# Mixture-of-experts routing: top two logits by max and max-index, routing weights behind the row numbers, slot table on POOL

## The reference, cut to what matters

```python
probs = softmax(x @ gate_w.T)                 # x: 2048 x 256, 8 experts
w, idx = top_k(probs, 2)
w = w / sum(w)
combine = zeros((2048, 8)).at[arange(2048)[:, None], idx].add(w)
for e in range(8):
    g, u = split(x @ gate_up[e].T, 2)         # 256 -> 2 x 1024
    out += combine[:, e:e+1] * (silu(g) * u @ down[e].T)
```

## Time and profile before

| | |
|---|---|
| median of 3 runs | 556.72 us (552.91 to 558.14) |
| span of the profiled execution | 555.4 us |
| PE busy | 495.3 us (89%), weight loads 363.6 us (65%) |
| DVE busy | 386.1 us (70%) |
| ACT busy | 340.2 us (61%) |
| POOL busy | 273.4 us (49%) |
| attention stage / routing / expert stage | about 233 / 33 / 289 us |

### The profile page before, as it was taken

How to read it: one execution, slowest core, us unless ns; L and a number is a source line. 1 busy time by engine, 2 the same in 40 slices (tenths; PEclk the granted TensorE clock), 3 DMA queues, 4 the chain that set the end, 5 groups by cost and what they waited for, 6 DMA issues and landing times.

```text
span 555.4 us, 12114 instructions
## 1 busy us (share of the span) xinstructions
PE 495.3 (89%) x3741; PEld 363.6 (65%) x3756; DVE 386.1 (70%) x805; ACT 340.2 (61%) x642; POOL 273.4 (49%) x347
## 2 busy tenths in 40 slices
PE   4695889998999888799798999999999999999990
PEld 3463546775666555526566888878888888777750
DVE  5437458888888765788577997887667677666551
ACT  1220588888788888374675777766656566645530
POOL 5006464574564564203227566656567555644244
PEclk9986799999999989899999999999999999999996
DMA  7567757768658632563666777967555465554224
GB/s 215 191 171 174 239 147 231 203 171 264 192 170 253 200 118 76 179 204 112 152 137 111 158 129 195 180 120 157 94 104 86 85 84 101 96 68 77 30 30 47
DMA packets 88090, 79.89 MB, mean 144 GB/s; under 512 B 49176, under 2 KB 73368, under 8 KB 87896
## 3 DMA queue, kind: packets, MB, share of 16 engines
q1 hardware_dynamic: 76512, 63.38, 41.8%
q0 software_dynamic: 11520, 15.74, 17.6%
HBM read 49.08 MB, written 22.41 MB: 129 GB/s over the span
## 4 chain that ended last, share of the span: by engine, by line
PE 67%; DVE 10%; ACT 7%; DMA 5%; issue 5%; SPq 3%; POOL 2%; another core or an unknown queue 0%; ACTq 0%; POOLq 0%
PE bank L1459 27%; PE bank L1476 13%; PE bank L1242 5%; PE bank L1288 4%; DMA x_parts<-WE 3%; PE bank L1274 3%; PE bank L1488 2%; PE bank L1256 2%; PE bank L1311 2%; PE bank L1324 2%; DVE FB L1165 2%; PE bank L1297 2%; DVE FB L1169 2%; ACT FB L876 2%; PE bank L1336 2%
## 5 line engine op out<-in xcount | busy, mean ns | idle before, releaser
L1459 PE MATMUL bank<-FB,WE 128*128 128x0 bf16 x1440 | 187.6, 280 | 2.6 <-issue 1.0
L1459 PEld LDWEIGHTS bank<-FB,WE 128*128 x1440 | 136.1, 98 | 34.9 <-issue 4.3
L709 POOL DMA_INDIRECT out<-FB,slot_tok x60 | 99.9, 1665 | 91.2 <-DVE FB L1186 85.4
L876 ACT ACTIVATE FB<-FB 128x512 bf16<-128x512 f32 x120 | 75.6, 630 | 69.9 <-DVE FB L1165 63.8
L1169 DVE TENSOR_TENSOR FB<-FB 128x512 bf16<-128x512 f32 x120 | 83.3, 694 | 46.9 <-ACT FB L876 43.0
L1476 PE MATMUL bank<-FB,WE 128*128 128x0 bf16 x720 | 103.7, 280 | 4.3 <-DVE FB L1169 2.2
L1165 DVE TENSOR_TENSOR FB<-FB,bank 128x512 f32<-128x512 f32 x120 | 81.9, 683 | 27.8 <-ACT FB L870 21.5
L700 POOL DMA_INDIRECT FB<-x_parts,slot_tok x60 | 61.7, 1028 | 68.0 <-DMA FB<-FB 26.7
L870 ACT ACTIVATE FB<-bank 128x512 f32<-128x512 f32 x120 | 70.7, 589 | 33.9 <-PE bank L1459 29.3
L1476 PEld LDWEIGHTS bank<-FB,WE 128*128 x720 | 67.6, 98 | 23.5 <-issue 7.8
L633 POOL TENSOR_TENSOR WE<-FB,WE 128x256 bf16<-128x256 f32 x104 | 67.8, 678 | 22.1 <-ACT WE L740 22.0
(11 more groups left out here) (180 smaller groups left out, 616.4 us busy)
## 6 DMA issues: line engine op xcount, KB each, us to landing
FB<-w SPq DMA_DIRECT2D x26, 512.0 KB, 5.5
WE<-w SPq DMA_DIRECT2D x44, 256.0 KB
WE<-q_parts SPq DMA_DIRECT2D x32, 200.0 KB
WE<-x SPq DMA_DIRECT2D x16, 256.0 KB, 5.2
q_parts<-FB SPq DMA_DIRECT2D x32, 128.0 KB
x_parts<-WE SPq DMA_DIRECT2D x20, 128.0 KB, 4.0
out<-WE SPq DMA_DIRECT2D x20, 128.0 KB, 5.5
q_parts<-WE SPq DMA_DIRECT2D x16, 128.0 KB
```

Of the source, the lines that this page charges most:

```text
L709: pool.indirect_dma_start(out=out, out_offset=bass.IndirectOffsetOnAxis(ap=slot_tok[:, c:c + 1].bitcast(U32), axis=0), in_=result_tile(c), ...
L876: nc.scalar.activation(hT[k % 3][:, 0, :], hid[k % 2], ACT.Copy).then_inc(hi_ready, 1)
L1459: ins = nc.tensor.matmul(to, wf[:, bass.ds(at + o, P)], xgT[s % 2][:, 2 * part + kc, :].shape_from_register(long[s % 2]), start=(z == 0), ...
```

## The change

1. Per tile, `logits` is not copied. DVE's `max` writes the eight logits in falling order and, behind a wait for it, `max_index` their indices (both from PSUM).
2. In the routing, one comparison of the first two indices with 0 to 7 gives both one-hot arrays at once, `r_oh`; their sum is the mask, now written in the order in which it is read from SBUF, with the reordering in PE's operand.
3. The triangular matrix holds -1 on and under the diagonal in place of 1 above it, so that the copy and one subtraction of the totals go. Both choices' products and sums are one instruction each. Position and tile come by a scaled conversion and a product in place of shift and mask; positions are centred about 0.
4. The routing weights (five instructions) move from behind the mask to behind the row numbers.
5. The slot table is made by POOL in 17 steps that start with `sizes_ready`, ahead of its wait for the row numbers; 13 DVE instructions go.
6. PE loads the table behind the second half of L1403, ahead of two units, and UNITS is (1, 7, 2, 2, 4, 1). PE's list is then: 1 unit, mask matmuls, 7 units, half of L1403, 2 units, the other half, table load, 2 units, L1410, 4 units, transposes of tiles 0 and 1, 1 unit, tiles 2 and 3.
7. A few constants are made differently, early in the attention stage.

```diff
...
-UNITS = (2, 10, 1, 1, 2, 1)
+UNITS = (1, 7, 2, 2, 4, 1)
...
             for i in range(TPB):
                 pool.wait_ge(xm_out[i], 16 * B)
                 pool.wait_ge(x2_out[i], 16 * B)
+            pool.wait_ge(sizes_ready, 1)
+            slot_no = r_iota[:, 0:NS].unsqueeze(2).broadcast_to([P, NS, E])
+            every = lambda v: v.unsqueeze(1).broadcast_to([P, NS, E])
+            step(nc.gpsimd.tensor_tensor(r_past, slot_no, every(r_end), ALU.subtract))
+            step(nc.gpsimd.tensor_scalar(r_past, r_past, 0.0, None, ALU.is_ge))
+            step(nc.gpsimd.tensor_tensor(r_here, slot_no, every(r_start), ALU.subtract))
+            step(nc.gpsimd.tensor_scalar(r_left, r_here, 0.0, None, ALU.is_ge))
+            step(nc.gpsimd.tensor_tensor(r_past, r_left, r_past, ALU.subtract))
+            step(nc.gpsimd.tensor_tensor(r_here, r_here, every(r_size), ALU.mult))
+            step(nc.gpsimd.tensor_tensor(r_left, every(r_inc[:, :, TT - 1]), r_here, ALU.subtract))
+            step(nc.gpsimd.tensor_tensor(r_left, r_left, every(r_size), ALU.subtract))
+            step(nc.gpsimd.tensor_scalar(r_left, r_left, 0.0, None, ALU.min))
+            step(nc.gpsimd.tensor_tensor(r_left, r_left, every(r_size), ALU.add))
+            step(nc.gpsimd.tensor_tensor(r_sums[:, 1], r_left, r_past, ALU.mult))
+            step(nc.gpsimd.tensor_tensor(r_sums[:, 0], r_past, r_rank.unsqueeze(1).broadcast_to([P, NS, E]), ALU.mult))
+            for n in (4, 2, 1):
+                step(nc.gpsimd.tensor_tensor(r_sums[:, :, :, 0:n], r_sums[:, :, :, 0:n], r_sums[:, :, :, n:2 * n], ALU.add))
+            step(nc.gpsimd.tensor_scalar(slot_at[:, 0:NS], r_sums[0:1, 0, :, 0], float(E - 1), float(EW), ALU.min, ALU.mult))
+            nc.gpsimd.tensor_scalar(slot_at[:, NS:2 * NS], r_sums[0:1, 1, :, 0], 1.0, float(CAP), ALU.max, ALU.min).then_inc(slots_ready, 1)
             pool.wait_ge(idx_ready, 1)
...
                     dve.wait_ge(lg_mm, n + 1)
-                    nc.vector.tensor_copy(logits[:, n, :], bank[bank_no("LG", n)][:, 0:E]).then_inc(lg_ready, 1)
+                    token_logits = bank[bank_no("LG", n)][:, 0:E]
+                    nc.vector.max(out=r_max[:, n, :], in_=token_logits).then_inc(top_ready, 1)
+                    dve.wait_ge(top_ready, n + 1)
+                    nc.vector.max_index(out=r_idx[:, n, :], in_max=r_max[:, n, :], in_values=token_logits).then_inc(lg_ready, 1)
...
             dve.wait_ge(lg_ready, TT)
-            dve.wait_ge(rconst_ready, 7 + len(CANDS))
-            prev = logits
-            for c, m in ((0, r_m1), (1, r_m2)):
-                step(nc.vector.tensor_reduce(m, prev, AX.X, ALU.max))
-                if c == 1:
-                    nc.vector.tensor_tensor(r_diff, r_m2, r_m1, ALU.subtract).then_inc(route_d, 1)
-                step(nc.vector.tensor_tensor(r_eq, prev, bc(m, E), ALU.is_equal))
-                step(nc.vector.tensor_tensor(r_key, r_eq, r_rank, ALU.mult))
-                step(nc.vector.tensor_reduce(r_top, r_key, AX.X, ALU.max))
-                step(nc.vector.tensor_tensor(r_oh[c], r_key, bc(r_top, E), ALU.is_equal))
-                if c == 0:
-                    step(nc.vector.scalar_tensor_tensor(out=r_two, in0=r_oh[0], scalar=-3.0e38, in1=logits, op0=ALU.mult, op1=ALU.add))
-                    prev = r_two
...
-            nc.vector.tensor_tensor(r_mask.rearrange("p e t -> p t e"), r_oh[0], r_oh[1], ALU.add).then_inc(route_m, 1)
-
-            dve.wait_ge(route_a, 1)
-            step(nc.vector.tensor_scalar(r_w[:, 0:TT], r_exp, 1.0, None, ALU.add))
-            step(nc.vector.reciprocal(r_w[:, 0:TT], r_w[:, 0:TT]))
-            step(nc.vector.tensor_tensor(r_w[:, TT:2 * TT], r_exp, r_w[:, 0:TT], ALU.mult))
-            step(nc.vector.tensor_copy(r_wh, r_w))
-            step(nc.vector.tensor_tensor(r_wl, r_w, r_wh, ALU.subtract))
+            dve.wait_ge(rconst_ready, 8 + len(CANDS))
+            chosen = r_idx[:, :, 0:2].rearrange("p t c -> p c t").unsqueeze(3).broadcast_to([P, 2, TT, E])
+            step(nc.vector.tensor_tensor(r_oh, r_rank.unsqueeze(1).unsqueeze(1).broadcast_to([P, 2, TT, E]), chosen, ALU.is_equal))
+            nc.vector.tensor_tensor(r_mask, r_oh[:, 0], r_oh[:, 1], ALU.add).then_inc(route_m, 1)
+            nc.vector.tensor_tensor(r_diff, r_max[:, :, 1], r_max[:, :, 0], ALU.subtract).then_inc(route_d, 1)
 
             dve.wait_ge(route_mm, 1)
             flat = lambda v: v.rearrange("p e t -> p (e t)")
-            step(nc.vector.tensor_copy(flat(r_tot), bank[1][:, 0:P]))
-            step(nc.vector.tensor_tensor_scan(flat(r_inc), flat(r_reset), flat(r_tot), 0.0, ALU.mult, ALU.add))
-            step(nc.vector.tensor_tensor(flat(r_slot), flat(r_inc), flat(r_tot), ALU.subtract))
-            step(nc.vector.tensor_tensor(flat(r_slot), flat(r_slot), bank[0][:, 0:P], ALU.add))
+            step(nc.vector.tensor_tensor_scan(flat(r_inc), flat(r_reset), bank[1][:, 0:P], 0.0, ALU.mult, ALU.add))
+            step(nc.vector.tensor_tensor(flat(r_slot), flat(r_inc), bank[0][:, 0:P], ALU.add))
...
-            step(nc.vector.tensor_scalar(r_base, r_start, float(CAP), None, ALU.mult))
+            nc.vector.tensor_scalar(r_base, r_start, float(CAP), -MIDDLE, ALU.mult, ALU.add).then_inc(sizes_ready, 1)
+            dve.wait_ge(sizes_ready, 1)
...
-            for c in range(2):
-                step(nc.vector.tensor_tensor(r_key, r_oh[c], r_slot.rearrange("p e t -> p t e"), ALU.mult))
-                step(nc.vector.tensor_reduce(r_sl[:, c * TT:(c + 1) * TT], r_key, AX.X, ALU.add))
-            step(nc.vector.tensor_copy(r_sli, r_sl))
-            step(nc.vector.tensor_single_scalar(r_tilei, r_sli, 7, ALU.arith_shift_right))
-            step(nc.vector.tensor_single_scalar(r_posi, r_sli, P - 1, ALU.bitwise_and))
+            step(nc.vector.tensor_tensor(r_key, r_oh, r_slot.rearrange("p e t -> p t e").unsqueeze(1).broadcast_to([P, 2, TT, E]), ALU.mult))
+            step(nc.vector.tensor_reduce(r_sl.rearrange("p (c t) -> p c t", c=2), r_key, AX.X, ALU.add))
             halves = lambda v: v.rearrange("p (g j) -> p g j", j=JL)
+            step(nc.vector.tensor_scalar(r_tilei, r_sl, 1.0 / P, None, ALU.mult))
             step(nc.vector.tensor_copy(r_tile, halves(r_tilei)))
-            step(nc.vector.tensor_copy(r_pos, halves(r_posi)))
+            step(nc.vector.scalar_tensor_tensor(out=r_pos, in0=r_tile, scalar=-float(P), in1=halves(r_sl), op0=ALU.mult, op1=ALU.add))
...
+            dve.wait_ge(route_a, 1)
+            step(nc.vector.tensor_scalar(r_w[:, 0:TT], r_exp, 1.0, None, ALU.add))
+            step(nc.vector.reciprocal(r_w[:, 0:TT], r_w[:, 0:TT]))
+            step(nc.vector.tensor_tensor(r_w[:, TT:2 * TT], r_exp, r_w[:, 0:TT], ALU.mult))
+            step(nc.vector.tensor_copy(r_wh, r_w))
+            step(nc.vector.tensor_tensor(r_wl, r_w, r_wh, ALU.subtract))
             for q in range(RG):
...
-            every = lambda v: v.unsqueeze(1).broadcast_to([P, NS, E])
-            slot_no = bc(r_iota[:, 0:NS], E)
-            step(nc.vector.tensor_tensor(r_past, slot_no, every(r_end), ALU.is_ge))
-            step(nc.vector.tensor_reduce(r_exf, r_past, AX.X, ALU.add))
...
-            nc.vector.tensor_scalar(slot_at[:, NS:2 * NS], r_lenf[0:1, :], 1.0, float(CAP), ALU.max, ALU.min).then_inc(slots_ready, 1)
             dve.wait_ge(route_mm, 3)
...
-            mask = r_mask.rearrange("p e t -> p (e t)")
+            mask = r_mask.rearrange("p t e -> p e t")
...
             ins.then_inc(route_mm, 1)
+            pe.wait_ge(slots_ready, 1)
+            at, length = slot_table()
+            set_length(0)
             differences(UNITS[3])
...
             turned_rows(1)
             differences(UNITS[5])
             turned_rows(2)
-            pe.wait_ge(slots_ready, 1)
-            at, length = slot_table()
-            set_length(0)
             turned_rows(3)
...
```

More of the change, by code:

```diff
@@ L162, in moe_attention_kernel @@
         et = lambda v: v.rearrange("p (e t) -> p e t", e=E)
[L163 to L165 removed]
+        r_key, r_oh = (rt(2 * TT * E).rearrange("p (c t e) -> p c t e", c=2, t=TT) for _ in range(2))
+        r_inc, r_slot, r_part = (et(rt(TT * E)) for _ in range(3))
         r_parti = et(rt(TT * E, I32))
@@ L176, in moe_attention_kernel @@
         r_tile, r_pos = (sm(2 * TT, F16).rearrange("p (g j) -> p g j", j=JL) for _ in range(2))
-        r_sli, r_tilei, r_posi = sm(2 * TT, I32), sm(2 * TT, I32), sm(2 * TT, I32)
-        r_nt, r_end, r_start, r_base, r_inv, r_size, r_gap, r_last = (rt(E) for _ in range(8))
+        r_tilei = sm(2 * TT, I32)
+        r_nt, r_end, r_start, r_base, r_inv, r_size, r_gap = (rt(E) for _ in range(7))
         r_sizei = rt(E, I32)
@@ L1415, in _ @@
             wf = WE[:, :, :].rearrange("p e n -> p (e n)")
-            long = [nc.tensor.shape_register(n) for n in range(2)]
             def turned_rows(i):
@@ L1424, in turned_rows @@
                 ins.then_inc(xgt_mm, 1)
```

(7 more changed lines are left out.)

60 lines of the change are left out of this document (32 added, 28 removed).

## The result

The changed kernel takes 561.56 us (median of 17 runs, 558.12 to 565.1), the kernel before beside it 558.48 us (17 runs). The ratio is 1.0072, 95% interval 1.0051 to 1.0093: 4.0 us slower, under the 1% that the prediction set as its bound for a change. (The two medians as they stand are 3.1 us apart, 0.55%.) 558.8 was forecast against a median of 556.72, so 2.1 us more; the kernel lost about twice that. The profiled execution spans 556.3 us (555.4 before).

A forecast was written before the change was run, and what follows sets the result against it. The prediction took TensorE's stream of units, not VectorE's chain of waits, as the bound. Attention +1.3 and routing +0.8 made +2.1 us on the median of 556.72: 558.8 us, range 553.2 to 563.0.

The forecast's parts named there:

- the units bound the stage: Last attention tile to first expert matmul: TensorE's 17 units of 1.1 to 1.3 us bound; 558.8 us, chance 0.52.
- the rival of a chain-bound kernel: Same stretch: VectorE's chain bounds, so row numbers 3.5 us earlier reach the first expert matmul; 553.8 us, chance 0.2.
- routing, +0.8: Mask to first expert matmul: despite earlier row numbers, the first expert matmul comes at 267.1 against 266.30, +0.8 us.
- Tables: VectorE's one-hot tables in routing: start at 244.6 instead of 248.72, quarters ready at 246.0, 247.4, 248.8 and 250.2.
- Clock: Two units between the row-number halves: 1.1 us each, 248.1 to 250.4, with no fall of clock charged.
- The load: TensorE's register load of the slot table: begins at 250.3, ends at 252.9, its hole of 1.7 us moved, not covered.
- The rest: TensorE behind the load: weights cost no wait, four units take 4.9 us, first expert matmul at 267.1.
- Rival C: Slot table on POOL: steps over 0.54 us each make TensorE wait for the table; at 0.75, 562.4 us; chance 0.12.
- attention, +1.3: Max and max-index per tile: 0.21 us more in each of six tiles ahead of the maxima, +1.3 us.
- rival D: Index search in attention is dear: 0.6 us a tile, 5.4 us in all, 562.9 us; chance 0.16.

The follow-up runs named there:

- e7: Changed kernel with slot table on VectorE, its load back ahead of the last transposes, and the old UNITS (2, 10, 1, 1, 2, 1); 1.0007 of the kernel before.
- e5: Changed kernel with slot table on VectorE, its load back ahead of the last transposes, and UNITS (1, 9, 2, 2, 2, 1); 1.0001 of the kernel before.
- e0: The changed kernel run once more, unaltered; 1.0071 of the kernel before.
- e3: Changed kernel with two more units ahead of the row-number matmuls, UNITS (1, 9, 2, 2, 2, 1); 0.9982 of the kernel before.
- e9: Changed kernel with only the slot table's load back ahead of the last transposes, POOL still making the table; 1.0061 of the kernel before.
- e1: Changed kernel with the slot table back on VectorE and its load back ahead of the last transposes; 1.0001 of the kernel before.
- e6: Changed kernel with POOL's steps held until VectorE's last table quarter stands, load back ahead of the last transposes; 1.0093 of the kernel before.
- e2: Kernel before with POOL's 17 steps added into unused scratch, VectorE still making the real table; 1.0032 of the kernel before.
- e4: Kernel before with MAX8 and the index search added behind the copy of the logits, results unused; 1.0016 of the kernel before.

## Why the prediction was right, and where it wasn't

**Right: the units bound the stage, not VectorE's chain.** VectorE's part of the change did what was worked out: the mask is ready at 234.38, the matmuls of the mask start as unit 0 ends, and the row numbers are written 1.1 us earlier than before even so. Nothing of it reaches the end. e7, which has the shorter chain and the old order, is at 1.0007; the rival of a chain-bound kernel asked for 0.993 to 0.996. Its wait of 1.23 us for the weight tables leaves some doubt; e5, which waits for a table only once, for 0.15 us, is at 32.4 us and 1.0001. The chain of waits, which named VectorE, showed the later of two nearly equal paths, as was argued.

**Wrong in size: routing, +0.8.** The stage grew by 2.5 us. Set against the forecast's own steps, with the 0.2 us by which the first unit started earlier counted in, the miss is 1.7:

- *Tables.* The first was to start at 244.6 and started at 245.15, and the second quarter was to be ready at 247.4 and was at 248.55. The unit behind it started at 249.06, not 248.1: 1.15 us with the offset. The price of each table was taken from rows in which POOL was idle; it runs beside POOL here. Counted from the first unit, the first table starts at 12.13 to 12.16 us in the four kernels with POOL's steps beside the changed chain (after, e0, e3, e9), and at 11.32 and 11.34 in e1 and e6, without them; the forecast had 11.4. So VectorE's own arithmetic was priced right, and POOL took 0.8 us from it ahead of the tables and 1.1 in them. That is the step that failed: the forecast asked of POOL's steps only whether they would be done in time, and not what they do to VectorE.
- *Clock.* Two units were charged with 2.3 us; they took 3.70 together, at a granted clock of 0.60 in that stretch. 1.4 us. The forecast had TensorE wait 1.0 us in this place (246.4 to 247.4) and left the clock alone; TensorE waited 2.59. Of that, 1.0 us is there because the seven units were through at 245.38 and not at 246.4, the clock having risen during unit 1; it moved nothing behind the wait.
- *The load.* It was to start at 250.3 and make a hole of 1.7. It started at 251.9, as the last quarter of the tables stood (251.83), and took 2554 ns, as before, but TensorE was late by then, so that it lay under the second half of the row numbers for longer: a hole of 0.97. That gave 0.7 back.
- *The rest* was right to 0.2: the weights wait for nothing, the four units take 4.8 us (4.9 charged), the last part 3.2 us from there (3.0 charged).

**Rival C was right in its condition and not in its path.** POOL's steps took 0.63 us each, over the 0.54 from which it was to decide, and ended at 251.66, behind the 250.3 at which TensorE was to want the table. Yet TensorE's last wait for VectorE's tables ended later, at 251.83, and the table cost less than expected. POOL's harm went through VectorE. The Trainium skill ("GPSIMD Engine Reference", section on engine selection) puts GpSimd at about half of VectorE's speed with two inputs. The forecast's estimate by that factor was 0.58 for a full step and an end at 250.8; the twelve steps from L703 to L714 average 0.58, and the end is 251.66. That the 0.58 came is luck. With VectorE idle such a step took 0.41 in e6, next to the forecast's own 0.42 and 1.5 times VectorE's 0.28 for 120 elements (L1141 of the kernel before); the one-input step behind it took 0.53, and the longer ones, up to 0.84, are found beside VectorE's. Nor did the rows that the forecast called in agreement show a factor of two: 678 ns against 0.58 us is 1.2.

**Wrong: attention, +1.3.** The index search is two instructions, 92 and 165 ns. With MAX8 ahead of them a tile takes 0.37 us from the first start to the maxima behind it (134.37 to 134.74), in place of 0.22 with the copy (134.53 to 134.75), and 0.34 to the statistics (141.96 to 142.30), in place of 0.05 (141.99 to 142.04). So ahead of the maxima, where it was charged, a tile costs 0.15 more and not 0.21, and in the other place 0.29 more. The Trainium skill ("VectorE: DVE Perf Modes", section on two Vector instructions with no wait between them) lists the search as those two instructions, and the trace agrees; the 0.42 made of it in the forecast didn't come, since the load, the search and the next instruction start 0.08 us apart. That it reaches the end isn't shown: the first unit starts between 232.4 and 237.4 in the nine profiles with the new attention stage, at 233.2 and 234.9 in the two with the old one. TensorE and its weight loads waited for the maxima 5.3 us (15 times) in place of 4.7 (11 times), which is 0.6, and the first unit starts no later. e1, with the whole new attention stage, is at 1.0001. By e1's interval, its stage being that of before, the term lies between -1.7 and 1.8 us; rival D's 5.4 is excluded.

So the forecast's answer, slower by less than 1%, held because a charge too many in one term (1.3) was nearly as large as what was missed in the other (1.7). The first isn't shown to cost anything, so that the answer came out is in part luck. What is left to the 4.0 us of the ratio isn't told by one profile; e0's has a stage 4.7 us longer than before, since the clock fell at another place there. Over all its runs e0 was granted a clock of 0.956 on average, the kernel before beside it 0.961; but in e9, with nearly the same loss, the two are 0.957 and 0.959, no further apart than noise. How much of the loss is waits and how much clock isn't known.

**Still open.** Why the clock falls behind one wait and not another: it fell after waits of 1.49 and 1.10 us (after) and held after 1.34 and 1.11 in the same kernel (e0), where it fell after a hole of 2.32; it fell after 1.20 (e2) and 1.23 (e7), and held after a hole of 2.33 (e3). With the hole of the load in its old place it held in the kernel before (1.34) and fell in e4 (1.26), so that no single execution tells what a wait costs. And what POOL and VectorE contend for: shown is that both slow down when they run together, not by what. The Trainium skill ("SBUF — State Buffer", section "Who interferes with whom") names a pair of SBUF ports for which a VectorE instruction with two SBUF inputs and a GpSimd instruction that reads SBUF contend, and calls it an exclusive lock. The trace agrees in that such instructions slow down (the table products, 692 to 786 ns, and POOL's steps, up to 0.84 us), and in one place in the order too: VectorE's L1120, begun at 243.01, kept its 0.60 us, and POOL's L707, begun under it at 243.15, took 0.78, where e6 has 0.44. Whether one is blocked whole or both share wasn't tried. No experiment gave a kernel clearly faster than before: e3's interval ends at 1.0015.

## What to carry to other kernels

Work moved to an idle engine is not free for the engine it leaves: price the instructions that will run beside it, not only its own end, and ask which of them another engine waits for. When a chain beside a full TensorE gets shorter, keep enough independent work ahead of the point where TensorE meets it; eight units where ten sufficed turned a harmless delay into a wait, and the wait in some executions into a lower clock. And before crediting time taken off the chain of waits, count the work that the other engines must do between the same two points.

## What the runs showed of the hardware

- POOL's elementwise steps and VectorE's slow each other in both directions. VectorE with two SBUF inputs: 692 to 786 ns (1024 f16 elements), 402 to 474 and 400 to 512 (480 f16), 400 to 576 (e6), 291 to 483 (L1114, 128 f32). With one input: L1123, 32 elements, 0.38 us where e1 has 0.18. POOL: the last step, 15 elements on one partition, 0.63 us beside VectorE and 0.30 with VectorE idle (e6). Not every VectorE instruction is slowed: L1116, 128 elements with two inputs, stayed at 0.29 in the midst of POOL's steps, and L1121, a sum over 256, at 0.42.
- A register load of 30 values from SBUF by TensorE's sequencer took 2.55 us each time, one of two values 0.72, and two of 14 in a row 3.68 and 1.34.
- MAX8 on 8 elements from PSUM took 161 ns, the load of the values to be matched 92 and the search 165; all three with the wait between take 0.34 to 0.37 us up to the start of the next instruction.
- The granted clock rises and falls at other moments in other executions of one kernel: the unit behind the mask took 1.22 us in one profile of the changed kernel and 1.58 in the other (e0), and the fall came behind the waits for the tables in the one and behind the hole of the load in the other.
